# Transposed operands from the host, the queries' norm folded into weight and exponent, and scores on four row groups, in a fused cross attention and ternary feed-forward kernel

## The reference, cut to what matters

```python
def xattn(q, ctx, Wq, Wkv, Wout):          # 16 heads of 16
    qp = q @ Wq.T
    k, v = split(ctx @ Wkv.T)
    scores = einsum(qh, kh) / sqrt(16)
    scores = where(tril, scores, finfo.min)
    out = softmax(scores) @ vh
    return out @ Wout.T
def ffn(x, w1, g1, w2, g2, w3, g3):
    # every linear: rmsnorm with gain, quantise to 8 bits by the token's maximum,
    # weight = round(tanh(w / mean|w|)) * arctanh(mean|w|)
    return linear(silu(linear(x, w1, g1)) * linear(x, w2, g2), w3, g3)
x = x + xattn(layernorm(x), ctx, Wq, Wkv, Wout)
x = x + ffn(layernorm(x), ...)             # hidden size 1024
```

## Time and profile before

| | us |
|---|---|
| time, median of 3 runs | 216.54 |
| time, lowest and highest of these runs | 214.63, 217.62 |
| profiled execution: span | 215.0 |
| DVE busy in it | 184.2 |
| PE busy in it | 170.9 |
| ACT busy in it | 152.4 |
| POOL busy in it | 143.6 |

### The profile page before, as it was taken

One profiled execution on the slowest core, in us unless ns is written; L12 is line 12 of the kernel. 1 busy time (PEld: TensorE's weight loads), 2 busy tenths in 40 slices (PEclk: granted clock), 3 DMA queues, 4 the chain that ended last, 5 costly groups with the idle time before them and its releaser, 6 DMA issues.

```text
span 215.0 us, 3666 instructions
## 1 busy us (share of the span) xinstructions
PE 170.9 (79%) x1073; PEld 110.0 (51%) x1080; DVE 184.2 (86%) x338; ACT 152.4 (71%) x218; POOL 143.6 (67%) x229
## 2 busy tenths in 40 slices
PE   4799877998997998999948878447489978788372
PEld 4755545585674865747436545124236544454251
DVE  2359799599999899997995889799999999999981
ACT  2355888958665896859864998829499968877622
POOL 5216292555667696886461666879899999999640
PEclk9999999999999999999997999959969999999979
DMA  6999000000000000000000000000000100010011
GB/s 163 340 377 361 27 3 2 0 2 5 0 0 3 0 0 0 0 0 3 2 0 0 0 3 0 0 2 0 30 24 24 49 24 24 24 52 24 24 49 49
DMA packets 8798, 9.09 MB, mean 42 GB/s; under 512 B 1488, under 2 KB 8400, under 8 KB 8784
## 3 DMA queue, kind: packets, MB, share of 16 engines
q1 hardware_dynamic: 8512, 8.65, 12.4%
q10 hardware_dynamic: 272, 0.26, 0.4%
HBM read 6.82 MB, written 2.10 MB: 41 GB/s over the span
## 4 chain that ended last, share of the span: by engine, by line
DVE 38%; issue 21%; PE 16%; ACT 12%; POOL 10%; DMA 2%; DVEq 1%; POOLq 0%; ACTq 0%
DVE hh L1195 5%; DVE probs L948 4%; DVE c_max L1213 4%; ACT q_x L819 4%; POOL u L384 4%; PE bank L555 3%; PE wide L511 3%; DVE m_x L1066 3%; DVE u_max L1059 3%; PE bank L706 2%; POOL half_sum L366 2%; DVE row_sum L955 2%; ACT hT L880 2%; DVE row_max L942 2%; PE bank L494 2%
## 5 line engine op out<-in xcount | busy, mean ns | idle before, releaser
L687 PE MATMUL wide<-wT,xqT 128*128 128x512 bf16 x128 | 33.5, 406 | 5.7 <-DVE hh L1195 3.5
L404 POOL TENSOR_TENSOR c_h<-hh,g3b 128x1024 f32<-128x1024 f32 x15 | 35.4, 2361 | 2.9 <-DVE hh L1195 2.5
L511 PE MATMUL wide<-k_diag,qT 128*128 128x512 f32 x64 | 28.9, 595 | 0.3 <-DVE k_diag L1000 0.3
L875 ACT ACTIVATE sq_junk<-hh,root_x 128x1024 bf16<-128x1024 f32 x16 | 18.4, 1147 | 15.2 <-DVE hh L1195 15.2
L706 PE MATMUL bank<-wT,hT 128*128 128x256 bf16 x128 | 17.6, 283 | 11.8 <-ACT hT L880 11.8
L334 POOL TENSOR_TENSOR k_diag<-kT,head_of 128x512 f32<-128x512 f32 x15 | 15.4, 1045 | 12.6 <-DVE kT L996 7.3
L819 ACT ACTIVATE q_x<-u,round_c,qs_x 128x256 f32<-128x256 f32 x32 | 16.6, 590 | 9.4 <-issue 5.1
L384 POOL TENSOR_TENSOR u<-xc,g 128x512 f32<-128x512 f32 x16 | 20.3, 1290 | 4.4 <-ACT q_x L819 4.4
L687 PEld LDWEIGHTS wide<-wT,xqT 128*128 128x128 bf16 (+1 forms) x128 | 12.3, 102 | 20.6 <-issue 7.3
L366 POOL TENSOR_TENSOR half_sum<-probs 128x512 f32<-128x512 f32 x16 | 20.1, 1277 | 3.4 <-ACT probs L779 3.3
L706 PEld LDWEIGHTS bank<-wT,hT 128*128 128x128 bf16 x128 | 11.6, 100 | 20.5 <-ACT hT L880 16.8
(11 more groups left out here) (139 smaller groups left out, 385.8 us busy)
## 6 DMA issues: line engine op xcount, KB each, us to landing
w_in<-in_L_ffn_w SPq DMA_DIRECT2D x3, 1024.0 KB, 10.3
out<-y SPq DMA_DIRECT2D x16, 128.0 KB, 1.7
x_sb<-in_x SPq DMA_DIRECT2D x1, 1280.0 KB, 12.4
x_sb<-in_x SPq DMA_DIRECT2D x1, 512.0 KB, 5.3
g3b<-in_L_ffn_g SPq DMA_DIRECT2D x1, 512.0 KB, 7.9
wq_in<-in_L_xattn_Wq ACTq DMA_DIRECT2D x1, 256.0 KB, 4.0
x_sb<-in_x SPq DMA_DIRECT2D x1, 256.0 KB, 3.6
wout_in<-in_L_xattn_Wout SPq DMA_DIRECT2D x1, 256.0 KB, 12.2
```

What stands on the lines that cost most here:

```text
L404: g.tensor_tensor(out=c_h[:, t, :], in0=hh[:, t, :], in1=g3b[:], op=ALU.mult).then_inc(c_ready, 1)
L511: last = nc.tensor.matmul(wide[:, n * 512:(n + 1) * 512], qT[:, c, t * P:(t + 1) * P], k_diag[:, c, :, :], start=(t == 1), stop=True)
L687: last = nc.tensor.matmul(wide[:, (w * 2 + n) * 512:(w * 2 + n + 1) * 512], xqT_cols(T, w * DC + c), w_cols[:, 4 * n:4 * n + 4, c, :], sta ...
```

## The change

The host hands over other layouts (`_layouts`): a second copy of x with features on the partitions (`xT`), the context transposed and doubled, and all weights transposed; for the query and key weights the features are also regrouped. PE's transposes of weights, context and normalised tokens, and the copies after them, go.

The norm of the queries' input is split. The mean is taken out of the query weight once (a matmul with ones sums its rows, DVE subtracts), and the reciprocal root multiplies the scores inside the exponential (`scale=ln_rstd`). `query` reads `xT`. `measure` and `aggregate` stay, but run ahead in groups: batches 1 and 2 in setup, 3 and 4 after iteration 0, 5 to 7 after iteration 1.

The scores use `k_pair`, two heads in 32 rows, 128 columns wide: 16 matmuls of 128 columns for a batch, each over 32 rows, four row groups that write to four banks. One signal tells that both tiles are done.

Orders move: DVE takes both maxima and the first shift ahead of the residual sum; ACT takes the exponential of a tile ahead of the copies of the next; POOL makes `v_pair` at the start of an iteration. ACT's absolute sums move out of setup to before iteration 0 (first weight) and after it (second and third). Tangents and rounding of the weights move to iterations 3 to 6 and lose their transposes. Two pairs of small DVE operations are cut differently (`scales_1`, `scales_4`).

The two `iteration` functions in the diff are ACT's (it begins with `recip_T_copy`) and DVE's (it begins with `sums`).

```diff
+                load_xT(0, 1).then_inc(xT0_in, 16)
+                sp.dma_start(ctxT[:], ctxT_d).then_inc(ctx_ld, 16)
                 load_x(0, 1).then_inc(x0_in, 16)
+                load_xT(1, 2).then_inc(xT12_in, 16)
                 load_x(1, 2).then_inc(x12_in, 16)
+                for i, w in enumerate((w1T_d, w2T_d, w3T_d)):
+                    sp.dma_start(w_in[:, i * WN:(i + 1) * WN], w).then_inc(w_ld[i], 16)
+                sp.dma_start(woutT[:], woutT_d).then_inc(wout_ld, 16)
+                load_xT(3, B - 3).then_inc(xT_in, 16)
                 load_x(3, B - 3).then_inc(x_in, 16)
...
                 def keys(b):
-                    need(pool, scores_done, 2 * b)
-                    for c in range(1 if isinstance(b, int) and b == 0 else DC):
-                        last = g.tensor_tensor(
-                            out=k_diag[:, c, :, :],
-                            in0=kT[:, c, bass.ds(b * SK, SK)].unsqueeze(1).to_broadcast([P, HPC, SK]),
-                            in1=head_of[:].unsqueeze(2).to_broadcast([P, HPC, SK]), op=ALU.mult)
-                    last.then_inc(kp_ready, 1)
+                    need(pool, scores_done, b)
+                    g.tensor_tensor(
+                        out=k_pair[:], in0=kT[:, :, bass.ds(b * SK, SK)].unsqueeze(2).to_broadcast([P, DC, 2, SK]),
+                        in1=half_of[:].unsqueeze(1).unsqueeze(3).to_broadcast([P, DC, 2, SK]),
+                        op=ALU.mult).then_inc(kp_ready, 1)
...
                 def scores(b):
                     need(pe, shifted, 2 * b)
+                    for r in range(PR):
+                        nc.tensor.matmul(wide[:, r * 512:r * 512 + 2 * P], ident_h[:], mask_h[:],
+                                         start=True, stop=True)
                     need(pe, qT_ready, b + 1)
                     need(pe, kp_ready, b + 1)
                     for t in range(TB):
                         for c in range(DC):
-                            n = t * DC + c
-                            last = nc.tensor.matmul(wide[:, n * 512:(n + 1) * 512], qT[:, c, t * P:(t + 1) * P],
-                                                    k_diag[:, c, :, :], start=(t == 1), stop=True)
-                        last.then_inc(scores_done, 1)
+                            for r in range(PR):
+                                rows, at = slice(32 * r, 32 * r + 32), r * 512 + (t * DC + c) * P
+                                last = nc.tensor.matmul(wide[:, at:at + P], qT[rows, c, t * P:(t + 1) * P],
+                                                        k_pair[rows, c, :, :], start=(t == 1), stop=True,
+                                                        skip_group_check=True)
+                    last.then_inc(scores_done, 1)
...
+                keep_warm(8)
                 pe.wait_ge(wq_ld, 16)
+                for kc in range(DC):
+                    last = nc.tensor.matmul(bank7[:, 0:D], ones[:], wqT[:, kc, :], start=(kc == 0), stop=(kc == DC - 1))
+                last.then_inc(wq_summed, 1)
...
+                def iteration(j):
                     if from_(j, 1):
                         recip_T_copy(j - 1)
-                    if live(j + 2):
-                        norm_T_copy(j + 2)
                     if from_(j, 3):
                         quantise(j - 3)
                     recip_widen(j)
                     probs_T_copy(j, 0)
                     if from_(j, 3):
                         tokens_T_copy(j - 3, bank5)
+                    if live(j + 1):
+                        exponentials(j + 1, 0)
                     probs_T_copy(j, 1)
+                    if live(j + 1):
+                        exponentials(j + 1, 1)
                     if live(j + 2):
                         query_copy(j + 2)
...
+                weight_sums(0)
+                iteration(0)
+                weight_sums(1)
+                weight_sums(2)
+                iteration(1)
+                iteration(2)
+                weight_tanh(0)
                 with act.Fori(3, 5) as j:
                     iteration(j)
+                weight_tanh(1)
                 iteration(5)
+                weight_tanh(2)
...
                 def iteration(j):
                     sums(j)
                     if from_(j, 1):
                         divide(j - 1)
-                    if live(j + 3):
-                        measure(j + 3)
                     maximum(j + 1, 0)
+                    maximum(j + 1, 1)
+                    shift(j + 1, 0)
                     if from_(j, 1):
                         residual(j - 1)
                         need(dve, bank4_free, j + 1)
-                    maximum(j + 1, 1)
-                    shift(j + 1, 0)
                     shift(j + 1, 1)
...
+                iteration(0)
+                dve.wait_ge(x_in, 16)
+                for b in (3, 4):
+                    measure(b)
+                    aggregate(b)
+                iteration(1)
+                weight_scales()
+                for b in range(5, B):
+                    measure(b)
+                    aggregate(b)
+                iteration(2)
+                arctanh_terms()
                 with dve.Fori(3, 5) as j:
                     iteration(j)
+                ternary(0)
                 iteration(5)
+                ternary(1)
```

417 lines of the change are left out of this document (156 added, 261 removed).

## The result

| | before | after |
|---|---|---|
| median of 15 runs each, us | 216.57 | 217.88 |
| lowest and highest | 214.63, 219.85 | 216.74, 218.78 |
| span of the profiled execution, us | 215.0 | 216.5 |

The ratio after to before is 1.009, with a 95% interval of 1.006 to 1.012. The forecast was 206.8 us, with a range of 201.5 to 213; the kernel became about 1% slower. The time of a run is 1.7 us more than its span. (Ratios compare executions of like kind, as those of the kernel before vary, so they need not be the ratio of two medians.)

The account below looks back on a forecast made before the run. DVE was taken to bound the steady attention iterations. A gain of 10.2 us less 0.5 for the clock takes 9.7 off the 215.0 span, giving 205.3; with 1.5 to the median, 206.8 us, range 201.5 to 213.

Parts of the forecast that it names:

- The clock: PE's rests of 2.3 to 4 us in iterations 0 to 3 lower its clock; 0.5 us allowed in all.
- the last stage: Feed-forward part, 72.7 us: claimed unchanged, so only the 142.3 us ahead of it could move.
- The sign named for it: Among the signs of a wrong forecast: PE's granted clock under 0.9 between 60 and 100 us.
- The first rival: Low clock for half of each iteration stretches PE's work to 14 us, so PE sets the pace: 222 us, chance 0.07.
- Iterations 0 to 2: Placing of the first three attention iterations: row sums of iteration 3 at 62.6 us, 6.6 sooner than before.
- the plan: Every instruction placed on paper in the new order; iteration 2 was planned at 14.2 us, the span without clock allowance 204.8.
- Iterations 3 to 6: Placing of the later attention iterations: row sums of batch 7 at 114.0 us, 10.2 sooner than before.
- covered by the same 3.6: Iteration 6: DVE's 2.54 us projection wait hidden by two maxima and a shift (3.6), leaving about 12.0 us.
- The stall in iteration 1: DVE stands from 34.2 to 36.6 us while ACT's two absolute sums delay the copy of the reciprocals.
- The residual sum of batch 5: Around iteration 5: comes without a wait, as 1.13 us of waiting for the projection goes.
- my 1.6: Estimated us for a batch's scores, 32 passes of 128 columns, between ends of 0.9 and 4.6.
- the second rival: Row groups don't run beside each other, scores take 4.6 us and PE passes DVE in iterations 3 to 6: 212.2, chance 0.13.

Follow-up runs that it names:

- f1_act_order: Changed kernel with ACT's queries' copy ahead of the second exponential and the logarithm last in iteration 5: 220.71 us from four runs of 216.44 to 221.94.
- the last variant: Changed kernel with arctanh operations early, ACT's row-scale waits moved, feed-forward filler matmuls, and scores of batch 3 made three times: 210.24 us, ratio 0.974 to the kernel before.
- e3_scores_3x: Changed kernel with masks and scores of batches 1 to 7 computed three times: 220.45 us, ratio 1.021 to the kernel before.
- h1_arctanh_early: Changed kernel with ACT's row-scale waits moved and DVE's twelve arctanh operations ahead of the three measures: 214.84 us, ratio 0.987 to the kernel before.
- g3_probs_T_again: Changed kernel with the second group of the first tile's probability transposes made four times in iterations 2 to 5: 216.81 us, ratio 1.002 to the kernel before.
- e2_warm_ffn: Changed kernel with filler matmuls in PE's rests of the feed-forward part: 215.37 us, ratio 0.996 to the kernel before.

## Why the prediction was wrong

**The step that failed is "The clock".** It saw the rests of 2.3 to 4 us and named their price, a projection of 3.6 to 3.8, rightly; it allowed 0.5 in all and looked no further than iteration 3. "Most of the slow work then lies under DVE's maxima" held for the attention part: 0.62 reached DVE in iteration 2, 1.07 in iteration 3 and some 0.5 in iteration 6, 2.2 together. What failed most is the sentence on the last stage, "there the change only reads the same weights in another order. So only the 142.3 us ahead of it can move": the same work took 4.3 more, and filler took 4.1 of it back. So the clock cost about 6 us in these profiles where 0.5 was allowed: 2.2 in the attention part, read as DVE's waits behind slow matmuls, and 3.5 to 4.1 in the feed-forward part, shown by filler. That it fell so heavily on the feed-forward part was not bound to come: in the profile of `f1_act_order` this part lost nothing. The sign named for it, a granted clock under 0.9 between 60 and 100 us, didn't even show in the changed kernel's profile: it was 0.91. The first rival, that the clock takes it all back, had the right direction, with 222 us, and the wrong mechanism: it had PE set the pace of every iteration. The price came from single matmuls that DVE waited for, and from a stage I had left out.

**"Iterations 0 to 2" missed two costs in iteration 2.** ACT's wait for the last row scales, 0.92, is in the code (`act.wait_ge(rstd_done, 4)` ahead of `iteration(2)`, a line that the excerpt of the diff above doesn't have), and I placed everything that ACT does but not what it waits for. And I took DVE's twelve small operations at 2.6, from a row in setup, where POOL does nothing beside them; beside POOL they took 3.7. For `m_x` I had seen a stretch beside POOL and did not carry it over. With the 0.62 of the clock these are 2.6 of the 3.0 that iteration 2 took over the plan.

**"Iterations 3 to 6": the 2.54 wait "covered by the same 3.6".** 1.27 of a wait remains in iteration 6 with PE at full clock, for the reciprocals of batch 6, which DVE now divides in the same iteration: the largest part of the +1.5 there. The rest of PE in iteration 5, behind ACT's logarithm, I had not placed either; the half clock behind it is the 0.5 named above.

**What held.** The first row sums came 1.0 late (PE's sums of the query weight took 2.07, where 0.9 was planned, and PE then waited 0.30 for the key weight). Iteration 0 was 9.52 for 9.5. The stall in iteration 1 came where it was put, 1.85 for 2.4, ended by the absolute sums. The first loop iteration without a clock loss is 12.1 for 11.9, and x was there in time. The residual sum of batch 5 had no wait, as foretold. In the last variant, with the causes removed, the span is 207.6 against a plan of 204.8; the 2.8 are setup 0.7, iterations 4 and 5 0.7, iteration 6 1.0, and 0.9 in iteration 3, passage and feed-forward, less 0.5 in iterations 0 to 2.

**The scores.** Row groups do run beside each other: 32 passes of 128 columns took 1.17 us, nearer to `weigh`'s 1.07 than my 1.6. At a granted clock of 0.50 they took 2.09. By the rule on weight loads that I quoted from the Trainium skill ("TensorE: Matmul & The Clock Gate", "LDWEIGHTS (loading the stationary operand)") they would have taken 4.6; the measurement decides against that reading of it. The Trainium skill's page "TensorEngine Tiling (Array Packing)", "Key Properties", says that different tiles load and multiply in parallel, and with that the trace agrees. So the second rival was false. In iterations 2 to 4 the scores' speed was worth nothing: with them made three times there, the kernel is faster. In iterations 0 and 6 it was worth 2.6 and 3.1 us (`e3_scores_3x`).

## What to carry to other kernels

When you take work away from PE in a kernel that another engine paces, ask where PE will rest, for the whole rest of the program: a later stage that the change doesn't touch can lose more than the changed one gains (here 4.25 against 2.75 us). Filler with no reader, in a bank that is free, is a cheap test of that, and here also the remedy. When instructions are placed on paper, place waits too, and take durations from a row that has the same neighbours on the other engines. A cost that you remove and get back some iterations later is no sign that it wasn't real; here there was a second cause behind it, and both had to go at once.

## What of the hardware was not expected

A DVE operation on 128x3 elements with two inputs took 1.16 us when it began 0.12 us after one of POOL's, and ended with it, against 0.16 with POOL at rest, and the chain of twelve 3.7 against 2.3 (`h1_arctanh_early`). The Trainium skill's page "SBUF — State Buffer", section "Who interferes with whom", says that a DVE instruction with two SBUF inputs contends with a GpSimd instruction that reads SBUF, that the port pair they share is an exclusive lock, and that issue order decides which of the two is blocked. The trace agrees: POOL began first, and DVE's operation ended at 66.25, within 0.05 us of the end of POOL's first instruction.

Projections behind rests of 3.09 and 3.94 us ran at 1.2 GHz (3.78 and 3.65 us), one behind 2.64 at 2.4 GHz (1.99, `g3_probs_T_again`). But a rest's length doesn't decide it alone: the last products of the kernel before ran at full clock behind the same rests of 1.21 us behind which those of the changed kernel ran at half. It differs even between executions of the same instructions. The projection in iteration 1, behind a rest of 1.78 us that no edit touched, in the changed kernel, in `e2_warm_ffn` and in `g3_probs_T_again`:

```profile
37.84 1.99 PE L523 MATMUL bank<-woutT,attnT 128*128 128x256 f32 x8 [1.78 <-DVE attnT L886]
...
37.25 3.31 PE L523 MATMUL bank<-woutT,attnT 128*128 128x256 f32 x8 [1.78 <-DVE attnT L896]
...
37.83 3.68 PE L524 MATMUL bank<-woutT,attnT 128*128 128x256 f32 x8 [1.78 <-DVE attnT L887]
```

So where a low stretch falls can't be read off one profile, and a kernel with many short rests of PE has to be looked at in several.
